# Layer 2 cross attention in 32-row blocks: scores in 64x32 tiles, probabilities turned on VectorE, outputs in 32x64 tiles

## The chip, the cores and the metric

One core of a Trainium2 chip runs the whole program. The metric is the device time of one execution in microseconds. The kernel is written in Bass: each engine has its own instruction stream, and the streams meet in semaphores only.

## The reference

Four layers work on x (8 batches x 256 tokens x 128). Each is a cross attention over 512 context rows and a feed-forward block. The change touches the cross attention of layer 2, with 16 heads of 64. In the reference's terms, for one batch:

```
q = layernorm(x) @ Wq.T                  # 256 x (16 heads x 64)
k, v = split(ctx @ Wkv.T)                # 512 x (16 x 64) each
s = q @ k.T * 64**-0.5 + key mask        # per head 256 x 512
p = softmax(s)                           # over the 512 keys
x = x + (p @ v) @ Wout.T + b_out
```

All of it is in f32. The result then goes through a layer norm into a local transformer ("l2a"), whose first tiles this stage already prepares (the LOCAL jobs).

## The kernel before, in words

The program is a list of phases, one after another. The one that matters is `wide_attention`, names ending in `_l2x`. Before it `l1_bit_ffn` already computes keys and values of batch 0 (`FirstPairs.product`, L1358), after it comes the local transformer.

**Units and steps.** One unit is one head by 128 queries: scores of 128x512. A batch has 32 units in 16 steps of two. The two units of a step are two heads that lie in partitions 0 to 63 and 64 to 127 of q and k, so their score products (L1987) use the two halves of PE's rows. Every engine runs the same order of steps, and works one step ahead: in step s PE issues the scores of s+1, DVE their maxima, ACT their exponentials.

**What a step does.** PE: `scores` of s+1, once DVE has read the two score banks `s_ps` of step s; `turn_probs` (L1996), eight 128x128 transposes of the probabilities of step s through the identity into `t_ps`; then the jobs of the step. DVE: `maxima` (L1771) adds the key mask, negates and keeps the row maximum; then it copies the turned probabilities into `pT` (L1844). ACT: `exponentials` (L1896), which also add up the row sums; then the drains of the jobs.

**Jobs.** They are PE work with a result in one of four ring banks, in an order written by hand in `next_batch` and `last_batch`: XT (turned x), Q, K and V (projections for the next batch, 4 + 8 + 8 jobs of 512 columns), PV (the output of a head pair, L1958: 8 products of 128 keys x 64, 256 columns, the two heads side by side in column halves), SUMS and SPREAD (inverse row sums, split in three bf16 parts on GpSimd, turned and spread over partitions), OUT (output projection, L1971). `fill` issues a job on PE, `drain` empties its bank, on ACT for all but SPREAD and OUT. A job waits until the job four before it is drained. q, k, v and the outputs `o` have two buffers each.

**The end.** After the last step there follow the last PV, SUMS, SPREAD and OUT, then moments, the power on GpSimd and the scaling for the next phase.

## Time and profile before

| | |
|---|---|
| runs | 1818.41, 1818.38, 1819.06 us; median 1818.41 |
| profiled execution | span 1816.4 us from first to last instruction; the median of the runs is 2.0 above it |
| mean granted TensorE clock | 0.941 of full speed |
| PE busy | 1613.7 us, 89% |
| DVE busy | 1299.2 us, 72% |
| ACT busy | 1049.8 us, 58% |
| POOL busy | 560.4 us, 31% |

PE is TensorE's matmul, PEld its weight load, DVE is VectorE, ACT ScalarE, POOL GpSimd. An f32 product appears as two matmul records and two weight loads, a transpose as one. Matmuls are pipelined and their ends are modelled, so what counts on PE is the distance from one start to the next. Layer 2 attention lies between 491 and 1067 us.

### The profile page before, as it was taken

Reading aid. Unit: us, or ns where it says so; the run is one execution under the profiler, and the core shown is the slowest. Engines: PE = TensorE matmul, PEld = TensorE weight load, DVE = VectorE, ACT = ScalarE, POOL = GpSimd, SP = SyncE. Lnnn points to the kernel's source line nnn. Section 1 sums busy time; section 2 is a strip of 40 time slices with the busy share of each in tenths; the row PEclk is TensorE's granted clock in tenths of the full one; section 3 lists DMA queues with packets and bytes.
Section 4 is the critical chain, followed back from the end, with each engine's and each line's share of the span. In section 5 each row is a group of like instructions: output and inputs, shape, how many; then the busy total and the mean of one; then the engine's idle time right before and its main releaser. Section 6 shows DMA issues by size and latency. Waiting matters only on the chain. (4 is left out here: it accounts for less than half of the span.)

```text
span 1816.4 us, 32822 instructions
## 1 busy us (share of the span) xinstructions
PE 1613.7 (89%) x11034; PEld 877.3 (48%) x11084; DVE 1299.2 (72%) x3515; ACT 1049.8 (58%) x2283; POOL 560.4 (31%) x634
## 2 busy tenths in 40 slices
PE   5876999996699999999999979997899986999976
PEld 3532344433355555555555546664566652333333
DVE  5636788866766666566666869976699856789847
ACT  2321666666655555555555549883489840677764
POOL 0306556421100000000000149944499612433210
PEclk9885999997799999999999999998899996899997
DMA  5124333201100000000000000001100001322100
GB/s 161 37 38 126 69 82 69 64 2 47 36 1 7 1 7 7 1 7 26 1 1 1 1 7 1 0 1 46 34 14 0 1 14 32 83 43 53 33 2 24
DMA packets 60239, 53.46 MB, mean 29 GB/s; under 512 B 9610, under 2 KB 52798, under 8 KB 59974
## 3 DMA queue, kind: packets, MB, share of 16 engines
q1 hardware_dynamic: 59238, 51.30, 11.8%
q8 instruction: 79, 1.29, 0.3%
q14 instruction: 58, 0.48, 0.1%
q10 hardware_dynamic: 864, 0.39, 0.1%
HBM read 30.57 MB, written 1.05 MB: 17 GB/s over the span
## 5 line engine op out<-in xcount | busy, mean ns | idle before, releaser
L1771 DVE CUSTOM_DVE_ANT_0 minus_s_l2x<-s_ps_l2x,mask_b_l2x 128x512 f32<-128x512 f32 x256 | 166.6, 688 | 175.8 <-PE s_ps_l2x L1987 175.7
L1896 ACT ACTIVATE probs_l2x<-minus_s_l2x,nmax_l2x 128x512 f32<-128x512 f32 x256 | 182.7, 714 | 178.2 <-DVE nmax_l2x L1771 178.1
L1069 DVE CUSTOM_DVE_ANT_0 junk_l1x<-s_ps_l1x,mask_b_l1x 128x512 f32<-128x512 f32 x256 | 166.3, 687 | 50.6 <-PE s_ps_l1x L1270 46.3
L1072 DVE TENSOR_REDUCE nmax_l3x<-s_ps_l3x 128x1 f32<-128x512 f32 x256 | 163.7, 683 | 32.4 <-PE s_ps_l3x L1270 30.4
L1131 ACT ACTIVATE pT_l1x<-st_ps_l1x 128x1024 f32<-128x1024 f32 x128 | 131.2, 1025 | 79.9 <-PE st_ps_l1x L1255 79.5
L1844 DVE COPY pT_l2x<-t_ps_l2x 128x512 f32<-128x512 f32 x256 | 164.3, 683 | 0.5 <-PE t_ps_l2x L1996 0.5
L1996 PEld LDWEIGHTS t_ps_l2x<-consts,probs_l2x 128*128 128x128 f32 x1024 | 109.6, 141 | 98.7 <-issue 78.1
L1996 PE MATMUL t_ps_l2x<-consts,probs_l2x 128*128 128x128 f32 x1024 | 139.8, 279 | 1.9 <-ACT probs_l2x L1896 1.9
L2582 POOL TENSOR_TENSOR rn_l2a_first<-ssc_l2a_first,consts 128x16 f32<-128x16 f32 x28 | 108.8, 3886 | 19.6 <-DVE ssc_l2a_first L2609 19.6
L2752 ACT ACTIVATE probs_l2a<-minus_s_l2a,nmax_l2a 128x128 f32<-128x128 f32 (+1 forms) x256 | 106.1, 424 | 8.8 <-DVE nmax_l2a L2657 8.7
L2538 POOL TENSOR_TENSOR v_l2x_first<-kT_l2x_first,tb_l2a_first 128x256 f32<-128x256 f32 x112 | 104.3, 963 | 4.8 <-ACT kT_l2x_first L2720 4.4
L2657 DVE CUSTOM_DVE_ANT_0 minus_s_l2a<-s_ps_l2a,consts 128x128 f32<-128x128 f32 (+1 forms) x256 | 67.5, 318 | 32.5 <-PE s_ps_l2a L2870 26.8
L1270 PE MATMUL s_ps_l3x<-kT_l3x_first,q_l3x 51*128 51x512 bf16 x192 | 74.6, 431 | 15.1 <-DVE nmax_l3x L1072 8.4
L1282 PE MATMUL pv_ps_l1x<-pT_l1x,v_l1x 128*32 128x256 f32 x1024 | 81.2, 391 | 1.0 <-ACT o_l1x L1139 0.9
L1131 ACT ACTIVATE v_l2x_first<-st_ps_l3x 128x1024 f32<-128x1024 f32 x64 | 65.2, 1024 | 23.3 <-PE st_ps_l3x L1255 23.3
L1131 ACT ACTIVATE kT_l2x_first<-st_ps_l3x 128x1024 f32<-128x1024 f32 x64 | 65.3, 1024 | 20.9 <-PE st_ps_l3x L1255 20.4
L1270 PE MATMUL s_ps_l1x<-kT_l1x_first,q_l1x 48*128 48x512 bf16 x192 | 66.3, 417 | 11.9 <-DMA q_l1x<-parts_l1x_first 8.5
L1987 PE MATMUL s_ps_l2x<-kT_l2x,q_l2x 64*128 64x512 f32 x256 | 72.3, 641 | 5.0 <-DVE nmax_l2x L1771 5.0
L1987 PE MATMUL s_ps_l2x<-kT_l2x_first,q_l2x 64*128 64x512 f32 x256 | 73.2, 649 | 3.0 <-ACT q_l2x L1874 1.5
L1723 POOL TENSOR_TENSOR out_rs_l2x<-out_ve_l2x,consts 128x2 f32<-128x2 f32 x8 | 5.7, 707 | 220.6 <-DVE out_ve_l2x L1803 220.6
L1242 PE MATMUL st_ps_l1x<-maskT_b_l1x,consts_bf 128*128 128x512 bf16 x215 | 68.1, 383 | 4.7 <-issue 3.2
L1255 PE MATMUL st_ps_l3x<-q_l3x,kT_l3x_first 54*128 54x256 bf16 x384 | 65.0, 282 | 0.0
(539 smaller groups left out, 3785.3 us busy)
## 6 DMA issues: line engine op xcount, KB each, us to landing
mask_i_l1x<-in_mask SPq DMA_DIRECT2D x8, 512.0 KB, 4.0
maskT_i_l1x<-in_mask_t SPq DMA_DIRECT2D x8, 512.0 KB, 4.9
...
```

Source lines behind the costliest of these rows:

```text
L1069: dve.tensor_tensor_reduce(out=junk[w][:], in0=s_ps[w][:], in1=mask_b[b % 2][:, j, :], scale=-1.0, scalar=3e38, op0=ALU.add, op1=ALU.min, ...
L1072: dve.tensor_reduce(to, s_ps[w][:], AX.X, ALU.max, negate=True).then_inc(m.s_drained[w].sem, 1)
L1131: act.activation(pT[t % 4][:, :, 2 * j:2 * j + 2, :].rearrange("p w c t -> p w (c t)"), st_ps[j][:], ACT.Exp)\
L1270: pe.matmul(s_ps[w][:], q[b % NST][rows, p, j * P:(j + 1) * P], kT[b % NST][rows, p, :], start=True, stop=True)\
L1771: dve.tensor_tensor_reduce(out=minus_s[n % 4][:], in0=s_ps[n % 2][:], in1=mask_b[b % 2][:], scale=-1.0, scalar=3e38, op0=ALU.add, op1=ALU. ...
L1844: dve.tensor_copy(pT[g % 2][:, hh, :, j * P:(j + 1) * P], t_ps[c % 2][:].rearrange("p (c t) -> p c t", t=P))\
L1896: act.activation(probs[n % 4][:], minus_s[n % 4][:], ACT.Exp, bias=nmax[:, b % 2, n:n + 1], scale=-1.0, accum_out=sums[:, b % 2, j, h:h + ...
L1987: pe.matmul(s_ps[n % 2][:], q[b % 2][rows, g, j * P:(j + 1) * P], kT[b % 2][rows, g, :], start=True, stop=True)\
L1996: ins = pe.transpose(t_ps[n % 2][:, c * P:(c + 1) * P], probs[n % 4][:, c * P:(c + 1) * P], k["ident"])
L2538: eng.tensor_tensor(other[:, j, w, :, to], qk[:, j, w, :, of], tb[:, w, j, to].unsqueeze(1).to_broadcast([P, NH, 32]), ALU.mult).then_inc( ...
L2582: pool.tensor_tensor(rn[:, cols], ssc[:, cols], k["minus_half"][:, 0:2 * NH], ALU.pow).then_inc(m.powers_ready.sem, 1)
L2752: act.activation(probs[n % (2 * DEEP)][:, cols], minus_s[n % (2 * DEEP)][:, cols], ACT.Exp, bias=nmax[:, u, TPB * n + j:TPB * n + j + 1], ...
```

## The change

- **Units.** A unit is now 32 queries of four heads (`BLK` = 32). A batch has two rounds of 8 heads; a round has 8 steps, one for each 32 queries; a step again two units of 128x512. Head c of a unit takes 32 partitions. A score group is 8 products in tiles of 64 rows x 32 columns.
- **Turning.** PE's transposes, the banks `t_ps` and their copies go. DVE turns each unit with one 32x32 block transpose from `probs` into `pT`. `minus_s` goes: maxima and exponentials work in `probs` itself, four buffers, so maxima wait for the transposes of the unit four before.
- **Outputs.** They no longer are ring jobs. `outputs(n, blocks)` multiplies for each of 16 blocks of 32 keys eight tiles of 32 rows x 64 columns, over the steps 1 to 7 of the next round (`blocks_of`), into four banks `pv_ps`.
- **Inverse sums.** GpSimd multiplies them with a 32x32 identity (512 columns), PE spreads them with a matrix of ones (8 products, 256 columns), ACT copies the result (`copy_inv`, 1024 columns), DVE multiplies the outputs with it (`normalise_outputs`, 1024 columns).
- **Values.** They are laid out by blocks of 32 keys: a V job is 16 products of 128 columns in tiles of 128 rows x 32 columns, also for batch 0 in the phase before.
- **Buffers.** q, kT, v and o have one buffer, the ring has two banks. Jobs K4 to K7, Q2, Q3 and V move into the batch that uses them.
- **Local jobs** move to the last batch's second half and behind it, and use other scratch tiles; OUT is split in two jobs of 128 tokens.

The core of the diff (left out are renamed signals, counts of semaphores and the passing of scratch tiles):

```diff
+    def project_values(self, pe, n, bank, ctxT):
+        r, part = divmod(n, 4)
+        for kb in range(4 * part, 4 * part + 4):
+            for c in range(4):
+                pair = 4 * r + c
+                ins = pe.matmul(bank[BLK * c:BLK * (c + 1), (kb % 4) * P:(kb % 4 + 1) * P], ctxT[:, BLK * kb:BLK * (kb + 1)],
+                                self.wv[:, pair * P:(pair + 1) * P], start=True, stop=True)
+        return ins
...
-    hd, G, NG = 64, 2, HEADS // 2
-    UNITS = HEADS * TPB
-    STEPS = UNITS // 2
-    RING = 4
-
-    XT, Q, K, V, PV, SUMS, SPREAD, OUT, LOCAL = range(9)
-    NQ, NV, NSPREAD = NG // 2, 2 * CPB, NG // 2
-    next_batch = {1: [(XT, 0), (K, 0), (K, 1)], 5: [(K, 2)], 6: [(K, 3)], 7: [(Q, 0), (Q, 1), (Q, 2)], 9: [(Q, 3), (K, 4), (K, 5)],
-                  11: [(K, 6), (K, 7), (V, 0)], 12: [(V, 1)], 13: [(V, 2), (V, 3), (V, 4)], 15: [(V, 5), (V, 6), (V, 7)]}
-    for_local = {2: [0], 4: [1], 5: [2, 3], 7: [4, 5], 9: [6], 11: [7]}
-    last_batch = {1: [(SUMS, 0)], 3: [(SPREAD, n) for n in range(NSPREAD)], 5: [(OUT, 0)]}
+    hd, NG = 64, HEADS // 2
+    ROUNDS = 2
+    NC = NG // ROUNDS
+    QB, KB = S // BLK, KV // BLK
+    STEPS = ROUNDS * QB
+    UNITS = 2 * STEPS
+    RING = 2
+    LAST = ROUNDS * B - 1
+    XT, Q, K, V, OUT, LOCAL = range(6)
+    NQ, NV = NG // 2, 2 * CPB
+    this_batch = {0: [(K, 4), (K, 5), (K, 6)], 1: [(K, 7)], 2: [(Q, 2)], 3: [(Q, 3)], 4: [(V, 0)], 5: [(V, 1)], 6: [(V, 2)], 7: [(V, 3)],
+                  14: [(V, 4), (V, 5)], 15: [(V, 6), (V, 7)]}
+    next_batch = {7: [(XT, 0)], 8: [(K, 0), (K, 1), (K, 2)], 9: [(K, 3)], 11: [(Q, 0)], 13: [(Q, 1)]}
+    last_batch = {10: [(OUT, 0)], 12: [(OUT, 1)]}
+    end_values = {8: [(V, 4), (V, 5)], 9: [(V, 6), (V, 7)]}
+    for_local = {10: [0], 11: [1], 12: [2], 13: [3], 14: [4], 15: [5]}
+    blocks_of = {1: range(0, 3), 2: range(3, 6), 3: range(6, 8), 4: range(8, 10), 5: range(10, 12), 6: range(12, 14), 7: range(14, 16)}
...
+        end = b + 1 == B
         jobs = [(f, b - 1, n) for f, n in last_batch.get(s, ()) if b > 0]
-        jobs += [(f, b + 1, n) for f, n in next_batch.get(s, ()) if b + 1 < B]
-        if s == 0 and b > 0:
-            jobs.append((PV, b - 1, NG - 1))
-        if s >= 2 and s % 2 == 0:
-            jobs.append((PV, b, s // 2 - 1))
-        if b + 1 == B:
+        own = end_values if end and s >= QB else this_batch
+        jobs += [(f, b, n) for f, n in own.get(s, ()) if b > 0 or f == Q]
+        jobs += [(f, b + 1, n) for f, n in next_batch.get(s, ()) if not end]
+        if end:
             jobs += [(LOCAL, b, n) for n in for_local.get(s, ())]
...
+    behind = [(LOCAL, B - 1, 6), (LOCAL, B - 1, 7), (OUT, B - 1, 0), (OUT, B - 1, 1)]
+    jobs = before + [job for b in range(B) for s in range(STEPS) for job in steps[b, s]] + behind
...
-        q = [sb(f"q{u}", [P, NG, S]) for u in range(2)]
-        kT = [first.kT, sb("kT1", [P, NG, KV])]
-        v = [first.v, sb("v1", [P, CPB, HEADS * hd])]
+        q, kT, v = sb("q", [P, NG, S]), first.kT, first.values
...
-        t_ps = [psum(m, ctx, f"t_ps{n}_l2x", [P, KV]) for n in range(2)]
+        pv_ps = psum(m, ctx, "pv_ps_l2x", [P, NC, 512])
...
+                def spread_inv(n):
+                    pool.wait_ge(*m.sums_inverted.after(n + 1))
+                    if n >= ROUNDS:
+                        pool.wait_ge(*m.pv_done.after(n - 1))
+                    pool.tensor_tensor(spread[n % ROUNDS][:], inv[:].unsqueeze(2).to_broadcast([P, 2 * QB, BLK]),
+                                       k["eye32"].unsqueeze(1).to_broadcast([P, 2 * QB, BLK]), ALU.mult).then_inc(m.inv_spread.sem, 1)
...
-                    for n in (2 * s, 2 * s + 1):
+                    for w in range(2):
+                        n = 2 * s + w
                         dve.wait_ge(*m.scores_ready.after(UNITS * b + n + 1))
-                        dve.tensor_tensor_reduce(out=minus_s[n % 4][:], in0=s_ps[n % 2][:], in1=mask_b[b % 2][:], scale=-1.0, scalar=3e38,
+                        if UNITS * b + n >= 4:
+                            dve.wait_ge(*m.turned.after(UNITS * b + n - 3))
+                        dve.tensor_tensor_reduce(out=probs[n % 4][:], in0=s_ps[w][:], in1=mask_b[b % 2][:], scale=-1.0, scalar=3e38,
                                                  op0=ALU.add, op1=ALU.min, accum_out=nmax[:, b % 2, n:n + 1]).then_inc(m.max_ready.sem, 1)
...
+                def turn_probs(b, s):
+                    r, qb = divmod(s, QB)
+                    n = ROUNDS * b + r
+                    if qb == 0 and n >= ROUNDS:
+                        dve.wait_ge(*m.pv_done.after(n - 1))
+                    for w in range(2):
+                        unit = 2 * s + w
+                        dve.wait_ge(*m.probs_ready.after(UNITS * b + unit + 1))
+                        dve.transpose(pT[r][:, w, :, BLK * qb:BLK * (qb + 1)], probs[unit % 4][:].rearrange("p (k t) -> p k t", t=BLK))\
+                            .then_inc(m.turned.sem, 1)
...
+                def normalise_outputs(n):
+                    rows = o[:, NC * (n % ROUNDS):NC * (n % ROUNDS + 1), :]
+                    dve.wait_ge(*m.inv_copied.after(n + 1))
+                    dve.tensor_tensor(rows, pv_ps[:, :, 0:S], rows, ALU.mult).then_inc(m.pv_copied.sem, 1)
...
-                                .then_inc(m.unit_copied[c % 2].sem, 1)
+                        turn_probs(b, s)
+                        if s % QB == 0 and n >= 2:
+                            normalise_outputs(n - 2)
+                        if s % QB == 0 and n >= 1:
+                            invert_sums(n - 1)
...
+                normalise_outputs(LAST - 1)
+                invert_sums(LAST)
+                dve.wait_ge(*m.scores_ready.after(UNITS * B))
+                local.rotate(dve, 0, empty_local)
+                local.sum_squares(dve, 1)
+                local.rotate(dve, 1, empty_local)
+                local.normalise(dve, 0)
+                normalise_outputs(LAST)
+                local.normalise(dve, 1)
...
+                def copy_inv(n):
+                    b, r = divmod(n, ROUNDS)
+                    act.wait_ge(*m.pv_done.after(n + 1))
+                    if b >= 1:
+                        for j in range(TPB):
+                            act.wait_ge(*full((OUT, b - 1, j)))
+                    act.activation(o[:, NC * r:NC * (r + 1), :], pv_ps[:, :, S:2 * S], ACT.Copy).then_inc(m.inv_copied.sem, 1)
...
+                        if s % QB == 0 and n >= 2:
+                            copy_inv(n - 2)
...
+                copy_inv(LAST - 1)
+                for job in behind[0:TPB]:
                     drain(job)
+                copy_inv(LAST)
...
-                    for n in (2 * s, 2 * s + 1):
-                        g, j, hh = unit(n)
-                        rows = slice(hd * hh, hd * (hh + 1))
-                        pe.matmul(s_ps[n % 2][:], q[b % 2][rows, g, j * P:(j + 1) * P], kT[b % 2][rows, g, :], start=True, stop=True)\
-                            .then_inc(m.scores_ready.sem, 1)
-
-                def turn_probs(b, s):
-                    pe.wait_ge(*m.probs_ready.after(UNITS * b + 2 * s + 2))
-                    for n in (2 * s, 2 * s + 1):
-                        if (b, s) > (0, 0):
-                            pe.wait_ge(*m.unit_copied[n % 2].after(STEPS * b + s))
-                        for c in range(CPB):
-                            ins = pe.transpose(t_ps[n % 2][:, c * P:(c + 1) * P], probs[n % 4][:, c * P:(c + 1) * P], k["ident"])
-                        ins.then_inc(m.turned.sem, 1)
+                    for w in range(2):
+                        rows = slice(hd * w, hd * (w + 1))
+                        for c in range(NC):
+                            g = NC * r + c
+                            ins = pe.matmul(s_ps[w][BLK * c:BLK * (c + 1), :], q[rows, g, BLK * qb:BLK * (qb + 1)], kT[rows, g, :],
+                                            start=True, stop=True)
+                        ins.then_inc(m.scores_ready.sem, 1)
...
+                def outputs(n, blocks):
+                    b, r = divmod(n, ROUNDS)
+                    for kb in blocks:
+                        if kb == 0:
+                            pe.wait_ge(*m.turned.after(2 * QB * (n + 1)))
+                            if n:
+                                pe.wait_ge(*m.pv_copied.after(n))
+                            for of in of_values(b, r):
+                                pe.wait_ge(*empty(of))
+                        for c in range(NC):
+                            for w in range(2):
+                                pe.matmul(pv_ps[hd * w:hd * (w + 1), c, 0:S], v[BLK * c:BLK * (c + 1), r, kb, hd * w:hd * (w + 1)],
+                                          pT[r][BLK * c:BLK * (c + 1), w, kb, :], start=(kb == 0), stop=(kb == KB - 1))
+                    if blocks[-1] == KB - 1:
+                        pe.wait_ge(*m.inv_spread.after(n + 1))
+                        for c in range(NC):
+                            for w in range(2):
+                                ins = pe.matmul(pv_ps[hd * w:hd * (w + 1), c, S:2 * S], k["ones"][BLK * c:BLK * (c + 1), 0:hd],
+                                                spread[r][BLK * c:BLK * (c + 1), QB * w:QB * (w + 1), :].rearrange("p q t -> p (q t)"),
+                                                start=True, stop=True)
+                        ins.then_inc(m.pv_done.sem, 1)
...
-                        turn_probs(b, s)
                         for job in steps[b, s]:
                             fill(job)
+                        if n >= 1 and s % QB in blocks_of:
+                            outputs(n - 1, blocks_of[s % QB])
+                outputs(LAST, range(KB))
```

## Rows read from the trace of the kernel before

**Rows 1.** The page: PE's busy time, share and instructions; the clock in 40 slices.

```profile
...
PE 1613.7 (89%) x11034; PEld 877.3 (48%) x11084; DVE 1299.2 (72%) x3515; ACT 1049.8 (58%) x2283; POOL 560.4 (31%) x634
...
PEclk9885999997799999999999999998899996899997
...
```

**Rows 2.** Windows by batch: busy us (x instructions) of each engine, clock, DMA share, GB/s.

```profile
...
629.00:700.00 71.00, 70.65 (x414) 39.77 (x412) 45.33 (x112) 38.73 (x94) 2.43 (x6) 1.00 0.02 5
...
1054.00:1067.00 13.00, 6.88 (x58) 5.82 (x58) 4.88 (x14) 0.64 (x2) 1.71 (x5) 1.00 0.00 0
sum 576.00, PE 559.84 PEld 316.30 DVE 375.77 ACT 306.09 POOL 28.17; mean PE 62.20 PEld 35.14 DVE 41.75 ACT 34.01 POOL 3.13
```

**Rows 3.** Groups by line and shape, PE, batch 2 (629 to 700).

```profile
...
L1987 PE MATMUL s_ps_l2x<-kT_l2x_first,q_l2x 64*128 64x512 f32 x64 | 18.1, 641 | 0.3 <-DVE nmax_l2x L1771 0.3
L1996 PE MATMUL t_ps_l2x<-consts,probs_l2x 128*128 128x128 f32 x128 | 17.5, 279 | 0.0
L1958 PE MATMUL ring_l2x<-pT_l2x,v_l2x_first 128*64 128x256 f32 x112 | 13.6, 385 | 0.0
...
L1971 PE MATMUL ring_l2x<-wo_l2x,o_l2x 128*128 128x128 f32 x32 | 3.7, 275 | 0.0
...
L1967 PE MATMUL ring_l2x<-invT_l2x,consts_bf 128*128 128x256 bf16 x8 | 1.0, 272 | 0.0
...
```

**Rows 4.** Order of time, PE, one step and the start of the next.

```profile
...
700.02 1.13 PE L1987 MATMUL s_ps_l2x<-kT_l2x,q_l2x 64*128 64x512 f32 x4
701.08 1.09 PE L1996 MATMUL t_ps_l2x<-consts,probs_l2x 128*128 128x128 f32 x8
702.01 2.74 PE L1954 MATMUL ring_l2x<-wv_l2x_first,ctxT_l2x 128*128 128x512 f32 x6
704.68 1.13 PE L1987 MATMUL s_ps_l2x<-kT_l2x,q_l2x 64*128 64x512 f32 x4
...
```

**Rows 5.** Order of time, all engines, the shortest step.

```profile
...
1044.01 1.13 PE L1987 MATMUL s_ps_l2x<-kT_l2x,q_l2x 64*128 64x512 f32 x4 [0.78 <-DVE nmax_l2x L1771]
...
1045.17 0.69 DVE L1771 CUSTOM_DVE_ANT_0 minus_s_l2x<-s_ps_l2x,mask_b_l2x 128x512 f32<-128x512 f32 x1
...
1045.90 0.72 ACT L1896 ACTIVATE probs_l2x<-minus_s_l2x,nmax_l2x 128x512 f32<-128x512 f32 x1 [0.74 <-DVE nmax_l2x L1771]
...
1046.40 1.28 DVE L1844 COPY pT_l2x<-t_ps_l2x 128x512 f32<-128x512 f32 x2
...
1046.53 1.13 PE L1987 MATMUL s_ps_l2x<-kT_l2x,q_l2x 64*128 64x512 f32 x4 [0.37 <-DVE nmax_l2x L1771]
...
1047.24 0.18 ACT L1896 ACTIVATION_READ_ACCUMULATOR probs_l2x<-minus_s_l2x,nmax_l2x 128x1 f32 x1
```

**Rows 6.** Order of time, PE, output products of layer 1's attention.

```profile
...
417.00 1.93 PE L1282 MATMUL pv_ps_l1x<-pT_l1x,v_l1x 128*32 128x256 f32 x32 [0.92 <-ACT o_l1x L1139]
...
```

**Rows 7.** Order of time, one 1024-column copy on ACT, one 1024-column product on DVE.

```profile
...
300.48 1.02 ACT L1131 ACTIVATE pT_l1x<-st_ps_l1x 128x1024 f32<-128x1024 f32 x1 [0.63 <-PE st_ps_l1x L1255]
...
1048.85 1.23 DVE L1590 TENSOR_TENSOR kT_l2x_first<-kT_l2x_first,rn_l2a_first 128x1024 f32<-128x1024 f32 x1
...
```

**Rows 8.** Groups by line and shape, ACT, batch 2.

```profile
...
L1896 ACT ACTIVATE probs_l2x<-minus_s_l2x,nmax_l2x 128x512 f32<-128x512 f32 x32 | 22.8, 715 | 22.2 <-DVE nmax_l2x L1771 22.2
...
L1876 ACT ACTIVATE kT_l2x<-ring_l2x 128x512 f32<-128x512 f32 x8 | 4.7, 590 | 3.6 <-PE ring_l2x L1951 3.5
...
```

**Rows 9.** Groups by line and shape, POOL, whole span.

```profile
...
L649 POOL TENSOR_TENSOR parts_l1x_first<-rest_l1x_first,parts_l1x_first 128x512 bf16<-128x512 f32 x7 | 8.1, 1158 | 0.6
...
```

**Rows 10.** Order of time, PE, the end of the stage.

```profile
...
1060.30 3.81 PE L1971 MATMUL ring_l2x<-wo_l2x,o_l2x 128*128 128x128 f32 x32 [2.19 <-DVE o_l2x L1787]
...
```

**Rows 11.** Windows of 5 us in the stage before.

```profile
...
460.00:465.00 5.00, 1.81 (x6) 0.38 (x5) 4.86 (x10) 5.00 (x11) 1.01 (x1) 0.97 0.00 0
465.00:470.00 5.00, 4.67 (x36) 3.51 (x37) 4.27 (x10) 4.76 (x6) 0.00 (x0) 0.69 0.00 0
...
```

More of the change, by code:

```diff
@@ L1366, in place, with place_values @@
             return self.kT[:, n, :]
-        c, half = divmod(n - self.JOBS // 2, 2)
-        return self.v[:, c, 512 * half:512 * half + 512]
+        return self.place_values(n - self.JOBS // 2)
+    def place_values(self, n):
+        r, part = divmod(n, 4)
+        return self.values[:, r, 4 * part:4 * part + 4, :].rearrange("p k e -> p (k e)")
     def close(self):
@@ L1630, in wide_attention @@
-    between = [(Q, 0, n) for n in range(1, NQ)]
+    before = [(XT, 0, 0), (Q, 0, 0), (Q, 0, 1)]
     steps = {(b, s): step_jobs(b, s) for b in range(B) for s in range(STEPS)}
-    behind = [(PV, B - 1, NG - 1), (SUMS, B - 1, 0)] + [(SPREAD, B - 1, n) for n in range(NSPREAD)] + [(OUT, B - 1, 0)]
-    jobs = before + between + [job for b in range(B) for s in range(STEPS) for job in steps[b, s]] + behind
+    behind = [(LOCAL, B - 1, 6), (LOCAL, B - 1, 7), (OUT, B - 1, 0), (OUT, B - 1, 1)]
+    jobs = before + [job for b in range(B) for s in range(STEPS) for job in steps[b, s]] + behind
@@ L1673, in wide_attention @@
         empty_local = lambda n: empty((LOCAL, B - 1, n))
-        last_four = lambda of: sorted(of, key=lambda job: number[job])[-RING:]
-        queries = lambda b: last_four([(Q, b, n) for n in range(NQ)] + [(K, b, g) for g in range(NG) if b > 0])
-        def unit(n):
-            g, rest = divmod(n, G * TPB)
-            return g, *divmod(rest, G)
+        last_two = lambda of: sorted((job for job in of if job in number), key=lambda job: number[job])[-RING:]
+        half = lambda f, b, r, n: [(f, b, i) for i in range(n * r // ROUNDS, n * (r + 1) // ROUNDS)]
+        of_scores = lambda b, r: last_two(half(K, b, r, NG) + half(Q, b, r, NQ))
+        of_values = lambda b, r: last_two(half(V, b, r, NV))
         def ahead(b, s):
@@ L1696, in _ @@
                     if b > 2:
-                        sp.wait_ge(*m.scores_ready.after(UNITS * (b - 2) + 4))
+                        sp.wait_ge(*full((V, b - 2, NV - 1)))
                     load_ctx(b)
@@ L1727, in _ @@
                 pool.wait_ge(*m.bias_loaded.after(16))
-                pool.wait_ge(*m.step.after(1))
-                for b in range(B):
-                    add_bias(b)
-                    if b >= 2:
-                        split_inv(b - 2)
-                        out_power(b - 2)
-                split_inv(B - 2)
-                out_power(B - 2)
-                for j in range(TPB):
-                    local.power(pool, j)
-                split_inv(B - 1)
+                add_bias(0)
+                add_bias(1)
+                for n in range(LAST + 1):
+                    if n >= 3 and n % 2 == 1:
+                        out_power((n - 3) // 2)
+                    if n == LAST:
+                        local.power(pool, 0)
+                    spread_inv(n)
+                    if n % 2 == 1 and n // 2 + 2 < B:
+                        add_bias(n // 2 + 2)
+                local.power(pool, 1)
                 out_power(B - 1)
@@ L1790, in drain @@
                         dve.wait_ge(*full(job))
-                        rows = x[:, TPB * b:TPB * (b + 1), :]
-                        dve.tensor_tensor(rows, bank(job)[:, 0:TPB * D].rearrange("p (t d) -> p t d", d=D), rows, ALU.add).then_inc(drains(job), 1)
+                        rows = x[:, TPB * b + j, :]
+                        dve.tensor_tensor(rows, bank(job)[:, 0:D], rows, ALU.add).then_inc(drains(job), 1)
                 def out_moments(b):
-                    dve.wait_ge(*empty((OUT, b, 0)))
+                    for j in range(TPB):
+                        dve.wait_ge(*empty((OUT, b, j)))
                     for t in range(TPB * b, TPB * (b + 1)):
@@ new lines, in _ @@
+                        if b + 1 == B and s == 14:
+                            local.sum_squares(dve, 0)
+                normalise_outputs(LAST - 1)
[7 more added lines that the diff above has]
+                local.normalise(dve, 1)
@@ L2025, in wide_attention @@
     local.close()
+    local.works_in_values()
 def l1_cross_attention(m):
```

207 lines of the change are left out of this document (76 added, 131 removed).

## The prediction

> **What bounds the kernel now.** The page comes first: PE is busy 89% of the span and its granted clock is near full over most slices [rows 1]. The change works in one stage, so the table of windows is next, cut where the scores of a new batch begin: layer 2 attention lasts 576 us, batches 1 to 6 take 71.0 us each to the tenth, and in those PE is busy 70.65 of 71 us at full clock, DVE 45.3 and ACT 38.7 [rows 2]. The stage is PE's work placed end to end. The PE groups of one batch [rows 3] and the order of time [rows 4] give its prices. Scores: 1.06 us from one start to the next group's (700.02 to 701.08), 0.2 of it a change of tile shape and a weight load that nothing covers. Eight transposes: 0.93. Three projection jobs: 2.67 to the next scores, 0.09 of it the array running empty before the shape changes, so 0.86 a job of two records; their row (2.74) outlasts 3 x 0.86 by 0.16, a modelled end. An output pair (16 records of 256 columns, two column tiles side by side): 8 passes of 0.215 (half a job's record) = 1.72, plus 0.15 to enter. Sum of a batch: scores 17.0, transposes 14.9, outputs 15.0, 20 K, V and Q jobs 17.2, output projection 3.7, inverse sums 1.3, turned x 0.4, 16 shape changes 1.4: 70.9 against 71.0 measured. So I trust the prices.
>
> **What goes.** PE loses the transposes (14.9 a batch) and the bf16 products that turned and spread the inverse sums (1.3 [rows 3]). DVE loses the copy of them (1.28 us for two, overlapped, so 0.61 from start to start [rows 5]); ACT loses eight output copies.
>
> **What PE gets.** (a) Scores: 8 tiles of 64 rows x 32 columns instead of 2 of 64x128, each with the same 512 columns to stream in two records. If all eight run side by side, as cheap as before: 1.06. (b) Outputs: for each block of 32 keys 8 tiles of 32x64, 256 columns, two passes of 0.215: 0.43 a block, 32 blocks 13.8 a batch, and 0.43 for each of two products that spread the inverses. (c) V jobs: 16 products of 128 columns in 128x32 tiles, four side by side: 8 passes of 0.11 = 0.88, as before. The nearest row: 16 products (32 records) of 128x32 tiles with 256 columns take 1.93 us [rows 6]. Less 0.16 of modelled end this is 4 x 0.44: four column tiles run fully in parallel in f32, their weight loads hidden. One after another they would need 32 x 0.215 = 6.9. Scores show two row tiles in parallel [rows 4]: 4 records in 1.06, two serial passes of 0.43. Rows and columns at once, and four row tiles in f32, no row shows. Bounds: all eight in parallel (226 us for scores, key blocks and inverses of the stage), or four at a time (452). I take all eight, since both directions are seen free at full size.
>
> The Trainium skill ("TensorE: Matmul & The Clock Gate", Part 3) says that a weight load overlaps running matmuls only if the row group differs; the four column tiles of a score share one. By that rule column tiles would go one by one; the third rival is that mechanism. The 1.93 us of [rows 6] are of tiles with one row group, and disagree with it.
>
> **The sum of a full batch.** 16 scores x 1.06 = 17.0; 16 changes out and in x 0.15 = 2.4; 20 jobs 17.3; output projection 3.6 and turned x 0.45; blocks and inverses 34 x 0.43 = 14.6; 14 entries to outputs x 0.15 = 2.1. Sum 57.5.
>
> **A new wait.** The ring has 2 banks instead of 4. Steps 0 and 8 issue three K jobs, and the third needs the first drained by ACT. ACT stands behind the next step's two exponentials, and in these steps also behind copy_inv. Times from the start of a step's scores, by a step that waits for nothing else (1044.01 [rows 5]): maxima from +1.16, exponentials from +1.89, second one ended +3.42; copy_inv over 1024 columns +1.03 [rows 7] gives +4.45; the drain of K +0.59 [rows 8] gives +5.05. Only then the third fill (0.86), so the next scores come at +6.05 instead of +3.75. That is 2.3 us on PE twice a batch; behind them on PE stand all scores, so DVE and ACT wait as well. 57.5 + 4.6 = 62.1, against 71.0.
>
> **Is DVE under this?** The shortest cycle is scores to scores through the maxima: 2.52 us (1044.01 to 1046.53 [rows 5]). In it DVE does two maxima (1.23) and two transposes. A 32x32 block transpose of 128x512 f32 stands in no row. The nearest is the 128x512 f32 copy at 0.61 us start to start; it reads PSUM, the transpose SBUF. Upper bound: two cycles for each element instead of one, about 1.2. I take 0.62. DVE then has 39.7 for maxima and transposes, 2 x 1.25 for the normalisation (the 1024-column product [rows 7]), 0.7 for reciprocals and some 4 for the rest: 47 of 62 us, covered by PE. In steps 0 and 8 it waits for copy_inv until +4.45 and is through at +6.1, just as the next scores start. GpSimd's spread of 512 columns (1.2 us [rows 9]) has six steps of time.
>
> The Trainium skill ("VectorE: DVE Perf Modes", The three transpose paths) gives 311 ns for 128x128 in bf16 and 32x32 blocks. At one element a cycle for the other 384 columns that is an estimate of 0.71 us, and the sum would be the same, as PE covers it.
>
> **The ends.** Batch 0 has its keys and values from the stage before, no outputs in its first half: eight cycles of 2.6 = 21, head 2.2 (the second Q job now comes before the first scores, at half clock), second half 24.8 (8 scores 8.5, six jobs 5.2, 17 blocks and inverse 7.3, changes 2.3, one wait without copy_inv 1.2, cycle floor 0.3): 48. Batch 7: no next batch (-5.6), local jobs (+4.4), shorter waits (-1.3): 59.6. Tail after the last step, where no scores cover anything: copy_inv and normalisation of the round before 2.4, 16 key blocks and inverses 7.5, then ACT takes two local drains before the last copy_inv (to +13.4), normalisation (+14.7), two output projections at 1.85 (half of 3.81 [rows 10]) to +18.4, add, moments, power and scale as now, 2.8: 21. Today's tail is 13 us [rows 2]. Stage: 48 + 6 x 62.1 + 59.6 + 21 = 501. Clock: 5 us with PE busy 1.81 are followed by a clock of 0.69 [rows 11]. Batch 0's first half is busy 43%, and round starts have idle gaps of 2.3; bound 0 to 20 us, I take 4. Stage 505 against 576: 71 us less. The other stages keep their work: the eight V jobs of the stage before keep their passes, local buffers only move.
>
> Span 1816.4 - 71 = 1745.4. The median of the runs, 1818.4, lies 2.0 above the span; 1747 us.
>
> **Rivals.** *Tiles four at a time* (slower side): each score +0.85, each block +0.43, 28.2 a full batch; 6 x 90.3, batch 0 at 69, batch 7 at 88, tail 28: 727, so 1973 us with the clock's 4. For it: no row has eight tiles. Against: [rows 4, 6]. It decides from 71 of 226 us more, that is when on average fewer than 6 of 8 tiles run together. Chance 0.12. *DVE becomes the bound*, transposes at 1.2: a step costs 1.23 + 2.4 = 3.63, a batch 58 + 7.5 = 65.5, batch 0 60, batch 7 65, tail 22: 540, with the clock 1792. Chance 0.08. *Column tiles one by one*, row tiles side by side: a score costs four times its two passes (+2.55), a block +0.43, a V job +2.6: 76 a full batch, the stage 1090, so 2335 us. For it nothing in the rows; against it [rows 6]. Chance 0.01. *More waits than counted* (two banks, one order on every engine, the clock at half in part of the stage): one us in every second step is 64 us, 1765 to 1811. Chance 0.09. *No change*: the waits eat all of it, one mechanism would have to cost 4.4 us a round; 0.02. Forecast 0.68, own range 1725 to 1765.
>
> **Range and chances.** From 1722 (the K wait shorter, no clock loss) to 1800, which takes in the DVE rival and most of the waits and leaves out the four-at-a-time rival. A measurement of this kernel tells 0.2%, 3.6 us, from no change. Faster 0.85, same 0.02, slower 0.13.
>
> **What would show it.** Right: score groups (16 or so records x 2) in 1.06 us and key blocks at 0.43; transposes near 0.62 us; full batches of 62 us with PE idle 2 us twice, released by ACT's drain of kT; a tail of 21. Wrong: score groups of 1.9 us, their records starting in four waves instead of two; DVE busy over 90% of a batch; PEclk below 1.0 inside the stage.

## The result, and the profile after

The changed kernel takes 1759.79 us (median of 4 runs, 1758.06 to 1760.49) beside 1818.39 for the kernel before (4 runs, 1816.62 to 1819.06): a ratio of 0.9678, 95% interval 0.9664 to 0.9692. The forecast was 1747.0, 13 us too low; the range held the time, and the sign was right. Its profiled execution has a span of 1758.5 us.

The page after: the engines' totals, the granted clock in 40 slices, and the groups of the new work. They answer to [rows 1, 3].

```profile
PE 1535.7 (87%) x16764; PEld 804.3 (46%) x16764; DVE 1303.6 (74%) x3513; ACT 1032.9 (59%) x2227; POOL 569.5 (32%) x618
...
PEclk9895999998869999999999899999999985899997
...
L1926 ACT ACTIVATE probs_l2x<-probs_l2x,nmax_l2x 128x512 f32<-128x512 f32 x256 | 182.8, 715 | 193.5 <-DVE nmax_l2x L1797 193.5
...
L1809 DVE STREAM_TRANSPOSE pT_l2x<-probs_l2x 128x512 f32<-128x512 f32 x256 | 166.4, 688 | 0.0
L2007 PE MATMUL s_ps_l2x<-kT_l2x_first,q_l2x 64*32 64x512 f32 x2048 | 147.5, 634 | 11.3 <-DVE nmax_l2x L1797 10.5
L2023 PE MATMUL pv_ps_l2x<-pT_l2x,v_l2x_first 32*64 32x256 f32 x4096 | 137.7, 385 | 2.6 <-issue 2.6
```

PE holds 50% more records and is busy 78 us less. The 2048 score records of 634 ns fill only 147.5 us, so the small tiles do run side by side. DVE's total barely moved: its copies of turned probabilities became block transposes of about the same length.

The windows by batch after, as in [rows 2]: batch 0, batch 2, batch 4, batch 7 and the tail, which is what follows the last step (columns: PE, PEld, DVE, ACT, POOL busy, clock, DMA share, GB/s).

```profile
492.00:543.20 51.20, 40.71 (x506) 13.06 (x506) 39.36 (x99) 27.82 (x71) 3.71 (x4) 0.77 0.01 2
...
603.30:668.30 65.00, 61.35 (x1127) 29.53 (x1122) 45.60 (x112) 36.24 (x88) 3.49 (x4) 0.95 0.02 7
...
731.80:793.60 61.80, 58.15 (x1132) 29.21 (x1125) 45.60 (x112) 36.28 (x88) 3.49 (x4) 1.00 0.02 7
...
917.20:981.70 64.50, 61.84 (x1240) 31.37 (x1232) 47.48 (x119) 39.32 (x92) 3.17 (x4) 0.97 0.01 3
981.70:1006.40 24.70, 16.40 (x316) 14.38 (x308) 17.69 (x32) 3.42 (x5) 8.93 (x4) 0.86 0.01 1
sum 514.40, PE 470.99 PEld 233.06 DVE 378.23 ACT 287.58 POOL 36.74; mean PE 52.33 PEld 25.90 DVE 42.03 ACT 31.95 POOL 4.08
```

The stage went from 576.0 to 514.4 us. The rest of the 57.9 us of span is small: the stage starts 1.0 later, and what follows it takes 752.1 instead of 749.4. Over all profiles of this case from here on, where the work outside the stage is the same or nearly so, the stage's start lay anywhere from 484.9 to 492.6 and the rest behind it took 748.5 to 752.1. Whole times of two kernels can differ by that alone, so I compare lengths of the stage.

Three of the full batches take 61.8, but batches 2 and 3 take 65.0 and 63.5 for the same work, with the clock at 0.95 and 0.97. Batch 4 has 3.65 us without PE. The order of time at its successor's start shows where:

```profile
794.61 1.95 PE L1373 MATMUL ring_l2x<-wv_l2x_first,ctxT_l2x_first 128*32 128x128 f32 x64
...
796.49 1.12 PE L2023 MATMUL pv_ps_l2x<-pT_l2x,v_l2x_first 32*64 32x256 f32 x32
...
797.97 0.18 PEld L2007 LDWEIGHTS s_ps_l2x<-kT_l2x_first,q_l2x 64*32 64x32 f32 x16 [0.39 <-issue]
797.97 1.09 PE L2007 MATMUL s_ps_l2x<-kT_l2x_first,q_l2x 64*32 64x512 f32 x16
...
798.99 1.98 PE L1988 MATMUL ring_l2x<-ctxT_l2x,wk_l2x_first 128*128 128x512 f32 x4
...
800.56 0.71 ACT L1926 ACTIVATE probs_l2x<-probs_l2x,nmax_l2x 128x512 f32<-128x512 f32 x1
...
801.26 1.00 ACT L1936 ACTIVATE o_l2x<-pv_ps_l2x 128x1024 f32<-128x1024 f32 x1
802.16 1.07 ACT L1910 ACTIVATE kT_l2x_first<-ring_l2x 128x512 f32<-128x512 f32 x2
...
802.80 1.13 PE L1988 MATMUL ring_l2x<-ctxT_l2x,wk_l2x_first 128*128 128x512 f32 x2 [1.82 <-ACT kT_l2x_first L1910]
...
803.85 1.09 PE L2007 MATMUL s_ps_l2x<-kT_l2x_first,q_l2x 64*32 64x512 f32 x16
```

PE's third K job waits for the first drain of K, which stands on ACT behind two exponentials and copy_inv. From the scores at 797.97: exponentials ended at +3.30, copy_inv at +4.29, the third K job starts at +4.83, the next scores at +5.88. I call this the K wait. Batch 2 shows the same wait and then this, in order of time and in two windows:

```profile
613.53 1.73 PE L2007 MATMUL s_ps_l2x<-kT_l2x_first,q_l2x 64*32 64x512 f32 x16
...
615.19 2.07 PE L1988 MATMUL ring_l2x<-ctxT_l2x_first,wk_l2x_first 128*128 128x512 f32 x2
...
618.67 1.09 PE L2007 MATMUL s_ps_l2x<-kT_l2x_first,q_l2x 64*32 64x512 f32 x16
```

```profile
612.47:613.53 1.06, 1.06 (x3) 0.30 (x3) 0.88 (x2) 0.43 (x1) 0.10 (x1) 1.00 0.00 0
613.90:617.20 3.30, 3.30 (x20) 0.51 (x4) 1.95 (x6) 1.54 (x4) 1.26 (x2) 0.50 0.00 0
```

The sixteen records that take 1.02 us to the next group elsewhere take 1.66 here, the one K job 2.07 instead of 1.13 for two records. The granted clock is still 1.00 (2.4 GHz) in the third K job and 0.50 (1.2 GHz) from 613.9 on, one job behind the idle time. The step is 5.14 us long instead of 3.56. Of the 13 K waits that stand behind copy_inv four are followed by such a step, two in batch 2, one each in batches 3 and 7.

The tail, in order of time, answers to [rows 10]:

```profile
984.37 7.17 PE L2023 MATMUL pv_ps_l2x<-pT_l2x,v_l2x_first 32*64 32x256 f32 x256 [2.57 <-issue]
...
991.30 0.67 PE L2029 MATMUL pv_ps_l2x<-spread_l2x,consts 32*64 32x256 f32 x16
...
994.41 1.02 ACT L1936 ACTIVATE o_l2x<-pv_ps_l2x 128x1024 f32<-128x1024 f32 x1
995.47 1.22 DVE L1822 TENSOR_TENSOR o_l2x<-pv_ps_l2x,o_l2x 128x1024 f32<-128x1024 f32 x1 [1.54 <-ACT o_l2x L1936]
...
996.74 6.79 PE L1993 MATMUL ring_l2x<-wo_l2x,o_l2x 128*128 128x128 f32 x32 [2.86 <-DVE o_l2x L1822]
...
1006.74 3.42 PE L2856 MATMUL ring_l2a<-consts,kT_l2x_first 128*128 128x128 f32 x16 [3.21 <-PEq L1709]
```

```profile
996.80:1002.90 6.10, 6.10 (x29) 6.10 (x30) 2.54 (x3) 0.00 (x0) 0.00 (x0) 0.50 0.00 0
1006.74:1009.80 3.06, 3.06 (x15) 3.06 (x16) 2.72 (x3) 1.43 (x3) 2.81 (x10) 0.50 0.29 88
```

The 32 records of the output projection took 3.81 before and take 6.79 now, at a granted clock of 0.50, behind 2.86 us without PE (2.19 before). The first 16 products of the next phase run at 0.50 too, and take 3.42 where they took 1.94.

### The profile page after: what moved, and what is told of

It reads as the page before. It is cut to its first block and busy times, and to the rows that moved or that the text cites. A ratio compares the mean times of both kernels' runs of the same rounds, so it can differ in the third digit from the quotient of the medians.

```text
span 1758.5 us, 44254 instructions
## 1 busy us (share of the span) xinstructions
PE 1535.7 (87%) x16764; PEld 804.3 (46%) x16764; DVE 1303.6 (74%) x3513; ACT 1032.9 (59%) x2227; POOL 569.5 (32%) x618
## 5 line engine op out<-in xcount | busy, mean ns | idle before, releaser
L1926 ACT ACTIVATE probs_l2x<-probs_l2x,nmax_l2x 128x512 f32<-128x512 f32 x256 | 182.8, 715 | 193.5 <-DVE nmax_l2x L1797 193.5
L1797 DVE CUSTOM_DVE_ANT_0 probs_l2x<-s_ps_l2x,mask_b_l2x 128x512 f32<-128x512 f32 x256 | 166.6, 689 | 120.5 <-PE s_ps_l2x L2007 120.1
L1809 DVE STREAM_TRANSPOSE pT_l2x<-probs_l2x 128x512 f32<-128x512 f32 x256 | 166.4, 688 | 0.0
L2007 PE MATMUL s_ps_l2x<-kT_l2x_first,q_l2x 64*32 64x512 f32 x2048 | 147.5, 634 | 11.3 <-DVE nmax_l2x L1797 10.5
L2023 PE MATMUL pv_ps_l2x<-pT_l2x,v_l2x_first 32*64 32x256 f32 x4096 | 137.7, 385 | 2.6 <-issue 2.6
L1740 POOL TENSOR_TENSOR spread_l2x<-inv_l2x,consts 128x512 f32<-128x512 f32 x16 | 17.6, 1101 | 324.5 <-DVE inv_l2x L1816 324.5
L2023 PEld LDWEIGHTS pv_ps_l2x<-pT_l2x,v_l2x_first 32*64 32x64 f32 x4096 | 79.9, 131 | 51.4 <-issue 37.2
L1134 ACT ACTIVATE v_l2x_first<-st_ps_l3x 128x1024 f32<-128x1024 f32 x64 | 65.2, 1024 | 24.3 <-PE st_ps_l3x L1258 24.3
L1134 ACT ACTIVATE kT_l2x_first<-st_ps_l3x 128x1024 f32<-128x1024 f32 x64 | 65.3, 1024 | 20.8 <-PE st_ps_l3x L1258 20.1
L1245 PE MATMUL st_ps_l1x<-maskT_b_l1x,consts_bf 128*128 128x512 bf16 x256 | 77.4, 384 | 0.0
L2945 PE MATMUL t_ps_l2a<-consts,probs_l2a 128*128 128x128 f32 x384 | 56.6, 284 | 4.7 <-ACT probs_l2a L2788 4.4
```

The lines of the kernel that those rows point to most:

```text
L1134: act.activation(pT[t % 4][:, :, 2 * j:2 * j + 2, :].rearrange("p w c t -> p w (c t)"), st_ps[j][:], ACT.Exp)\
L1797: dve.tensor_tensor_reduce(out=probs[n % 4][:], in0=s_ps[w][:], in1=mask_b[b % 2][:], scale=-1.0, scalar=3e38, op0=ALU.add, op1=ALU.min, a ...
L1809: dve.transpose(pT[r][:, w, :, BLK * qb:BLK * (qb + 1)], probs[unit % 4][:].rearrange("p (k t) -> p k t", t=BLK))\
L1926: act.activation(probs[n % 4][:], probs[n % 4][:], ACT.Exp, bias=nmax[:, b % 2, n:n + 1], scale=-1.0, accum_out=sums[:, r, w, qb:qb + 1]). ...
L2007: ins = pe.matmul(s_ps[w][BLK * c:BLK * (c + 1), :], q[rows, g, BLK * qb:BLK * (qb + 1)], kT[rows, g, :], start=True, stop=True)
L2023: pe.matmul(pv_ps[hd * w:hd * (w + 1), c, 0:S], v[BLK * c:BLK * (c + 1), r, kb, hd * w:hd * (w + 1)], pT[r][BLK * c:BLK * (c + 1), w, kb, ...
```

## The experiments

Theory: the stage is PE's work at the prices forecast (57.5 us a full batch), plus the K wait, plus time at the lower clock. Rivals: the small tiles cost more than full ones, or DVE (74% busy) holds PE up, or something else would end as late as the K wait, so that nothing is won without it. Every kernel ran beside the kernel before, whose medians were 1818.52 to 1820.54.

**The inverse copy first.** ACT copies the inverses ahead of the next step's exponentials, as soon as the products that spread them are done. The drains of K then stand behind the exponentials alone.

```diff
+                        if s % QB == 0 and n >= 2:
+                            copy_inv(n - 2)
                         if ahead(b, s)[0] < B:
                             exponentials(*ahead(b, s))
-                        if s % QB == 0 and n >= 2:
-                            copy_inv(n - 2)
```

> ACT issues copy_inv ahead of the next step's exponentials instead of behind them; nothing else changes. My theory (the third K job of steps 0 and 8 waits for a drain that stands behind two exponentials AND copy_inv): the drain comes 1.03 us earlier in 13 rounds, those steps fall from 5.88 to about 4.85 us, 13 us in all, so about 1746 against 1760. Rival (two banks alone make the wait, copy_inv only fills idle time of ACT): 1760. Second rival (the exponentials are now late, and DVE and PE behind them): 1760 or more.

Measured 1737.77 us, ratio 0.9563 (0.9532 to 0.9594), the stage 495.5. In order of time:

```profile
785.29 1.02 ACT L1936 ACTIVATE o_l2x<-pv_ps_l2x 128x1024 f32<-128x1024 f32 x1
...
788.41 1.05 ACT L1910 ACTIVATE kT_l2x_first<-ring_l2x 128x512 f32<-128x512 f32 x2
...
789.03 1.12 PE L1988 MATMUL ring_l2x<-ctxT_l2x,wk_l2x_first 128*128 128x512 f32 x2 [0.91 <-ACT kT_l2x_first L1910]
...
790.09 1.09 PE L2007 MATMUL s_ps_l2x<-kT_l2x_first,q_l2x 64*32 64x512 f32 x16
```

PE's idle time fell from 1.82 to 0.91 and the step from 5.88 to 4.97: ACT's order is the cause of that half of the wait. Batches 2 to 6 take 59.99 each. 14 waits shorter by 0.91 (13 behind K, one behind V in batch 7) are 12.7 us, and the four steps at half clock are gone as well (6.4 us). Together 19.1; the stage lost 18.9. The expectation had only the first, and was 8 us too high.

**K jobs dealt 2, 1, 1** instead of 3, 1 over the steps 0, 1, 2 and 8, 9, 10, with the jobs behind them moved on. The two ring banks then suffice in steps 0 and 8.

```diff
-    this_batch = {0: [(K, 4), (K, 5), (K, 6)], 1: [(K, 7)], 2: [(Q, 2)], 3: [(Q, 3)], 4: [(V, 0)], ...
+    this_batch = {0: [(K, 4), (K, 5)], 1: [(K, 6)], 2: [(K, 7)], 3: [(Q, 2)], 4: [(Q, 3), (V, 0)], ...
-    next_batch = {7: [(XT, 0)], 8: [(K, 0), (K, 1), (K, 2)], 9: [(K, 3)], 11: [(Q, 0)], 13: [(Q, 1)]}
+    next_batch = {7: [(XT, 0)], 8: [(K, 0), (K, 1)], 9: [(K, 2)], 10: [(K, 3)], 11: [(Q, 0)], 13: [(Q, 1)]}
```

> K jobs of steps 0, 1 and 8, 9 are laid out 2, 1, 1 instead of 3, 1 (Q2, Q3 a step later), so no step needs a third bank. My theory: PE's wait of 2.1 us on the K drain goes, but DVE stands in front of copy_inv until +4.45 and is through with normalising at +5.9, 1.8 us later than the next maxima are due, so a wait of DVE takes its place and only 1.1 us of a round is won: 15 us, about 1745. Rival (the K drain is the whole wait): 2.1 x 14 = 29 us, 1731.

Measured 1736.05 us, ratio 0.9547 (0.9515 to 0.9579), the stage 494.2, batches 59.58.

```profile
783.67 1.09 PE L2007 MATMUL s_ps_l2x<-kT_l2x_first,q_l2x 64*32 64x512 f32 x16
...
785.06 1.22 DVE L1822 TENSOR_TENSOR o_l2x<-pv_ps_l2x,o_l2x 128x1024 f32<-128x1024 f32 x1 [0.67 <-ACT o_l2x L1936]
785.56 1.12 PE L1988 MATMUL ring_l2x<-ctxT_l2x,wk_l2x_first 128*128 128x512 f32 x2 [0.80 <-ACT kT_l2x_first L1910]
...
786.61 1.55 PE L2023 MATMUL pv_ps_l2x<-pT_l2x,v_l2x_first 32*64 32x256 f32 x48
...
788.10 1.09 PE L2007 MATMUL s_ps_l2x<-kT_l2x_first,q_l2x 64*32 64x512 f32 x16
```

Step 0 falls to 2.93 us, but the next one is 4.43 where 3.56 would do: its K job still finds ACT late by 0.80 with copy_inv. So a part of the wait moved on one step: two of 0.87 a batch, in place of two of 2. Neither side of the expectation holds. What took the K wait's place is ACT's drain once more, not a wait of DVE, and it took less than half of the gain.

**Both edits.**

> Both edits together. My theory: neither PE nor DVE then waits at a round's start, 2.0 us a round, 28 us, and with the long gaps of PE gone also some of the steps that run at the lower clock: 1726 to 1732, full batches of 58 us. Rival (the two edits cure the same wait): as the better of the two alone, 1745.

Measured 1725.42 us (1713.23 to 1726.31), ratio 0.9495 (0.9469 to 0.9521). The profile is of the run of 1713.23: its stage started at 484.9 and took 478.0. Timed again (below) the kernel took 1726.16, and its stage started at 492.6 and took 481.8. The window of a full batch of the second profile:

```profile
608.50:666.30 57.80, 57.80 (x1129) 29.16 (x1122) 45.03 (x113) 36.24 (x88) 3.49 (x4) 1.00 0.03 7
```

PE is busy all of 57.80 us. With no wait left a full batch is within 0.3 us of what the prediction's count of work gave, 57.5.

**TensorE kept at work.** Products into banks not in use, whose results nobody reads: 4 in each of steps 1 to 7 of batch 0, and 29 in the tail's gaps.

```diff
                             fill(job)
+                        if b == 0 and 1 <= s < QB:
+                            stay_awake(m, pe, pv_ps[:, 0, :], 4)
...
+                pe.wait_ge(*free(behind[0]))
+                stay_awake(m, pe, bank(behind[0])[:], 9)
                 outputs(LAST, range(KB))
...
```

> Products whose result nothing reads keep PE working where it had gaps: four of 512 bf16 columns in each of steps 1 to 7 of batch 0, and 9, 10 and 10 of them in three gaps of the tail (before the last outputs, before the first output projection, behind the second). My theory (the halved clock in batch 0 and in the tail costs 3 us each, and 1.5 us at the start of the next phase): batch 0 from 51.2 to about 48, the last output projections from 6.8 to 3.8 us, 5 to 8 us in all, 1752 to 1755. Rival (these stretches are set by DVE and ACT, not by PE's clock): 1760.

Measured 1752.01 us, ratio 0.9625 (0.9598 to 0.9652), the stage 512.9. Batch 0 fell from 51.3 to 47.9. The time from the last scores to the end of the stage fell from 30.3 to 27.4. But seven steps behind a K wait now ran at the lower clock instead of four (batches 1 to 4), three more at 1.6 each, which took back 4.8. That makes the 1.5 us by which the stage is shorter. Of the 8.2 us between the two profiles 1.1 more lie behind the stage, where the next phase's first products take 1.94 again, and 5.6 before it, where both kernels do the same. So the time fell into the expected 1752 to 1755 by luck: the expectation had no slow steps in it, and most of the gain in the profile isn't the extra products' doing.

**Extra turns.** In batches 0 to 6 every step makes one more block transpose, into scratch.

```diff
+                        if w == 0 and b + 1 < B:
+                            dve.transpose(scratch[0][:, 0:KV].rearrange("p (k t) -> p k t", t=BLK), probs[unit % 4][:].rearrange("p (k t) -> p k t", t=BLK))
```

> DVE does one block transpose more in each step of batches 0 to 6, into a scratch tile that nothing reads: 112 x 0.61 = 68 us more of DVE's work, and the result stays whole. My theory (PE sets the pace, DVE has 15 of 62 us to spare in a batch): 5 us more in the first half of batch 0, where the cycle through DVE is the floor, and about 1 us in each full batch, 1765 to 1775. Rival (DVE is as good as the bound): 1820 or more.

Measured 1759.21 us, ratio 0.9673 (0.9639 to 0.9707). One of the four executions took 5096 us, nothing on record says why, and the ratio leaves it out; the other three took 1757.55 to 1759.51. Windows of batch 2 and batch 4:

```profile
603.90:665.70 61.80, 58.16 (x1130) 29.22 (x1122) 54.90 (x129) 36.26 (x88) 3.48 (x4) 1.00 0.03 7
730.70:795.70 65.00, 61.35 (x1130) 29.59 (x1122) 54.89 (x129) 36.26 (x88) 3.48 (x4) 0.95 0.02 7
```

DVE has 9.3 us more in 61.8 (54.9, 89% of the window) and a batch at full clock is as long as before. DVE is not the bound of a full batch; the expectation of a few us, for steps that run at DVE's cycle, holds in batches 0 and 1 alone (53.1 and 60.9 instead of 51.3 and 60.0). Steps at the lower clock are now in batches 3, 4 and 5, two in each. The stage is 519.0 long, 4.6 more than without the extra turns. That the two kernels' times agree is luck: the stage started 2.0 us earlier in this profile, and what follows it took 3.4 less.

**Four tiles instead of eight in a key block.** Left out: the second 64-column tile of every row group in key blocks 1 to 14 of 16, so half of their value products.

```diff
-                            for w in range(2):
+                            for w in range(1 if 0 < kb < KB - 1 else 2):
```

> The changed kernel without the output products of the second head of each pair, except in the first and last key block: 14 of 16 blocks issue 4 tiles instead of 8, so these outputs are incomplete. My theory (eight tiles run side by side): a block takes 0.43 us either way, 1760, 0 to 3 us less. Rival (PE pays for each product, even a little): 14 x 16 blocks x 0.2 = 45 us less, 1715.

Measured 1749.22 us, ratio 0.9628 (0.9609 to 0.9647), the stage 505.8. Three blocks are 48 records in the changed kernel. Here they are 32, in order of time:

```profile
798.78 1.54 PE L2023 MATMUL pv_ps_l2x<-pT_l2x,v_l2x_first 32*64 32x256 f32 x32
800.25 1.09 PE L2007 MATMUL s_ps_l2x<-kT_l2x_first,q_l2x 64*32 64x512 f32 x16
```

They take 1.54 us and 1.47 to the next scores; the 48 records at 786.61 above take 1.55 and 1.49. A full batch is 61.48 instead of 61.81: eight tiles cost what four cost, and the rival is out. The expectation missed the rest. Of the 8.6 us that the stage lost, 6.4 are the four slow steps: no step behind a K wait ran at the lower clock here, though the wait is as long as ever.

**Block transposes in the kernel before.** In the kernel before, PE's transposes and the copies give way to one 32x32 block transpose per unit on DVE. Left out: the blocks are not moved to where a 128-row product wants them, so its probabilities are not fully turned; units, tiles, ring and buffers stay.

```diff
-                            dve.wait_ge(*m.turned.after(UNITS * b + c + 1))
-                            dve.tensor_copy(pT[g % 2][:, hh, :, j * P:(j + 1) * P], t_ps[c % 2][:].rearrange("p (c t) -> p c t", t=P))\
+                            dve.wait_ge(*m.probs_ready.after(UNITS * b + c + 1))
+                            dve.transpose(pT[g % 2][:, hh].rearrange("p c t -> p (c t)").rearrange("p (k t) -> p k t", t=2 * P)[:, :, j * P:(j + 1) * P], probs[c % 4][:].rearrange("p (k t) -> p k t", t=P))\
...
-                        turn_probs(b, s)
```

> The kernel before with one part of the change alone: DVE turns the probabilities in 32x32 blocks out of SBUF, PE's transposes are gone, and scores, outputs, jobs, ring and buffers stay. The blocks stay within their 32 partitions, so the outputs of the attention are not the reference's; instructions and sizes are. My theory (a full batch is PE's work end to end): 14.9 us of transposes and 1.4 us of shape changes go from each of 8 batches, less where a step falls under the floor of 2.5 us: 56 to 58 us a batch, 1818 - 110 = 1700 to 1715. Rival (DVE's transposes cost as much as PE's did): 1818. The distance to 1760 is then the price of the 32-row layout with one buffer and two banks.

Measured 1726.85 us, ratio 0.9501 (0.9486 to 0.9517), the stage 483.6. A full batch of it:

```profile
600.60:658.80 58.20, 56.05 (x286) 26.42 (x284) 45.27 (x113) 36.97 (x95) 2.44 (x6) 1.00 0.02 5
```

71.0 to 58.2 is what taking the transposes off PE is worth: 12.8 us a batch. PE's work fell by 14.6 (70.65 to 56.05), and 2.15 us of PE idle came up in its place. The expectation, 1700 to 1715, had taken the whole 16.3 in every batch. The layout of 32 queries, which makes the block transpose usable, costs 3.6 us a full batch over that. The K wait is 4.0 of it (61.8 against 57.8 without it). The small tiles are not free: PE works 57.8 against 56.05, but this fills idle time that the other kernel has. A larger price of the layout lies at the end. From the last scores to the end of the stage it takes 30.3 us, this kernel 20.8 and the kernel before 20.5, as the last round's 16 key blocks come when no scores are left to cover anything.

**All three edits,** beside the two again, on one chip:

> The changed kernel with all three edits: the inverse copy ahead of the next exponentials, the K jobs dealt 2, 1, 1, and the extra products in batch 0 and in the tail that keep TensorE at work. Theory (the K wait and the granted clock are two separate losses, so they add up): batch 0 near 47 us instead of the 49.3 of the two edits alone, full batches 57.8 as there, the tail 22 to 24, the stage near 474 instead of 478, and 3 to 6 us below the kernel with the two edits, 1719 to 1722. Rival (with no K wait left the clock has nothing to lose in batch 0, and the extra products are only work in the way): the same time as with the two edits, 1723 to 1727.

> The kernel with the two edits (inverse copy first, K jobs dealt 2, 1, 1) beside the one with the extra products, on the same chip: 1725 by its first timing, which spread from 1713 to 1726. Both theories expect that again; what it says is how large a difference of 3 to 6 us to the other kernel is worth.

Measured 1714.99 us (1712.09 to 1716.16), ratio 0.9431 (0.9415 to 0.9447), and 1726.16 (1724.73 to 1726.95), 0.9496 (0.9481 to 0.9511). The stage is 474.0 and 481.8. In order of time, the tail with all three, and windows of batch 0, batch 7 and the tail:

```profile
945.63 7.17 PE L2023 MATMUL pv_ps_l2x<-pT_l2x,v_l2x_first 32*64 32x256 f32 x256 [0.52 <-issue]
...
958.00 3.84 PE L1993 MATMUL ring_l2x<-wo_l2x,o_l2x 128*128 128x128 f32 x32 [0.69 <-DVE o_l2x L1822]
```

```profile
490.70:537.70 47.00, 41.12 (x535) 14.05 (x539) 39.40 (x99) 27.66 (x72) 3.71 (x4) 0.93 0.01 2
...
882.80:943.10 60.30, 60.26 (x1240) 31.31 (x1234) 47.23 (x120) 39.50 (x92) 3.31 (x4) 1.00 0.01 3
943.10:964.70 21.60, 19.45 (x334) 13.91 (x336) 17.45 (x32) 3.28 (x5) 8.78 (x4) 1.00 0.01 2
```

Wait and clock are two items: with no K wait left the extra products still shorten the stage by 7.8 us, 4.5 in batch 0 and 3.3 behind the last scores. That is more than expected, as the kernel with two edits had a batch 0 of 51.5 in this profile (49.3 in its first). Of the 11 us between the two medians, 2.0 in the profiles lie before the stage, where the kernels are the same, and 1.3 behind it. This is the fastest version, 104 us under the kernel before on this chip.

**The changed kernel and the one with four tiles once more.**

> The changed kernel once more, for its steps at half clock. In its first profile batches 2, 3 and 7 held steps of 5.1 to 5.2 us behind the K wait where the others took 3.56. Theory (the wait of 2.1 us puts the clock at risk, and whether it falls varies from one execution to the next): again 1758 to 1761 us, some such steps, but perhaps in other batches. Rival (something fixed in those batches' work lowers it): the same batches 2, 3 and 7.

> The kernel with four tiles instead of eight in 14 of 16 key blocks once more, on the same chip. It keeps the K wait. Theory (chance from one execution to the next): some steps of 5.1 to 5.2 us behind the K wait this time. Rival (with less work around the wait the clock stays up): none again, every full batch 61.5 us, and a time near 1749.

Measured 1757.85 us (0.9656, 0.9636 to 0.9675) and 1746.55 (0.9607, 0.9587 to 0.9627). My theory that chance decides fell: the second profile of the changed kernel has its slow steps in the same places, 5.16 and 5.21 in batch 2, 5.20 in batch 3, 5.14 in batch 7 (5.14, 5.21, 5.21, 5.13 in the first), and the kernel with four tiles has none in either. The low stretches start at 613.8 and 612.5 in the two profiles of the changed kernel, both 121.8 us behind the stage's first scores. The rival, something fixed in the work of batches 2, 3 and 7, doesn't hold either: with extra products or extra turns the same waits in other batches are the slow ones.

## Why the prediction was right, and where its sum was off

- **Tiles side by side: right.** Scores in 1.02 us (forecast 1.06), key blocks at 0.43 (16 in 6.93 from 984.37 to 991.30), two V jobs in 1.88. The four-at-a-time rival (28.2 us a batch) and the one-by-one rival are out by the rows, and by the kernel with four tiles. The Trainium skill ("TensorE: Matmul & The Clock Gate", Part 3) has weight loads overlap running matmuls only between row groups. The four column tiles of a score share one, and the trace disagrees: all 16 loads are through in 0.18 us (the PEld row at 797.97), while the products of the first pass already run. That column tiles would go one by one was the prediction's own inference from that rule.
- **Work of a full batch: right.** 57.5 forecast, 57.8 measured without a wait (the kernel with two edits).
- **The K wait: right in place and cause, a little smaller.** Next scores at +6.05 forecast, +5.88 measured. The forecast's own terms, 5.05 and 0.86, give +5.91. Two waits and the work make 61.8, against 62.1.
- **Transposes: right.** 0.69 us busy each, two of a step in 1.30 as they overlap, and DVE is covered: 45.6 of 61.8 us, forecast 47. The DVE rival is out, since 9.3 us more in a full batch cost nothing. (Its price was added up wrongly: a stage of 540 and 4 for the clock give 1786, not 1792.)
- **Clock, "0 to 20, take 4": the term most undersized.** It cost about 13 in the stage: 3.4 in batch 0 (51.3 against 47.9 with TensorE kept at work), 1.58 + 1.65 + 1.65 + 1.57 = 6.4 in four steps behind the K wait, 3.1 in the tail (24.7 against 21.6). I had put it at batch 0 and the round starts, and took a size near the low end of my bound; that the tail's own waits would halve the clock for the output projection (6.79 us where I counted 3.7) is in no term. A clock below 1.0 inside the stage was one of the prediction's own signs of being wrong, and it showed: 0.77 in batch 0, 0.95, 0.97 and 0.97 in batches 2, 3 and 7, 0.86 in the tail. It is also one of the conditions of the rival with more waits than counted (1765 to 1811); the other waits of that rival did not come.
- **Batch 7: undersized.** 64.5 against 59.6. Its work without waits is 60.3, where I had 56.3 (57.5 - 5.6 + 4.4). The count missed two V jobs of batch 6 that spill into it (320 records of L1373 instead of 256, 1.7 us), two key blocks and a spread product (1.3) and the turning for the local jobs (1.7). These busy times make 4.7, 0.7 more than the difference; what makes up for that is not shown. Waits and clock added 4.2.
- **Sum.** Batch 0 +3.3, batches 1 to 6 +1.3 (373.9 against 372.6), batch 7 +4.9, tail +3.7, less the 4 set aside for the clock: +9.2 of the 9.4 by which the stage is over 505. The other 3.7 us of the span's 13.1 are the later start and the phases behind. 1.5 of them are the next phase's first products at the lower clock; for the rest I had allowed no spread.

By cause: the clock 13 instead of 4 is the 9 us. The 4.0 of work missed in batch 7 are balanced, by luck, by the full batches (0.3 less in each of batches 2 to 6: waits 0.6 shorter, work 0.3 more), by 0.7 less of waits in batch 7, and by batch 1, which took 60.0 as its first step has no V jobs.

What stays open is why some K waits of 1.8 us bring the clock down and others of the same length don't. Waits of 0.8 and 0.9 us never did, in the full batches of the two kernels that had them. The places were the same in two executions of a kernel and move when its timing moves (batches 1 to 4, or 3 to 5), so when a wait comes matters and not only how long it is; no run here isolates what decides it.
